# Turning v with identity products and placing half of the sums' head blocks on POOL, in a fused Mamba, cross-attention and ternary-FFN block

## The reference, cut to what matters

```python
xn   = rmsnorm(x);  proj = xn @ w_in.T                # val, gate (256 each), B, C (16 heads x 128), dt (16)
val  = silu(causal_conv4(val));  dt = softplus(dt + bias);  ld = -exp(A_log) * dt
cum  = cumsum(ld)                                     # per chunk and head
L    = exp(cum[l] - cum[m]) where l >= m, else 0
Y    = ((C @ B.T) * L) @ val_heads + D * val          # 16 heads of 16 channels
out  = (Y * silu(gate)) @ w_out.T                     # then a decayed associative memory read, residual
x    = layernorm(x + attn);  x = layernorm(x + cross_attention(x, ctx, mask))
x    = layernorm(x + bitlinear(silu(depthwise_conv3(bitlinear(x)))))
```

## Time and profile before

| | us |
|---|---|
| median of 3 runs | 879.39 (878.04 to 880.06) |
| the profiled execution, whole | 878.6 |
| its span, first to last instruction | 876.8 |
| TensorE busy in the span | 818.3 (93%) |
| VectorE, ScalarE, GpSimd busy | 723.8, 738.7, 166.3 |
| mean granted TensorE clock, share of full | 0.976 |

### The profile page before, as it was taken

One profiled execution on the slowest core, in us unless ns is written; L12 is line 12 of the kernel. 1 busy time (PEld: TensorE's weight loads), 2 busy tenths in 40 slices (PEclk: granted clock), 3 DMA queues, 4 the chain that ended last, 5 costly groups with the idle time before them and its releaser, 6 DMA issues.

```text
span 876.8 us, 19690 instructions
## 1 busy us (share of the span) xinstructions
PE 818.3 (93%) x7051; PEld 570.0 (65%) x7051; DVE 723.8 (83%) x2189; ACT 738.7 (84%) x1409; POOL 166.3 (19%) x198
## 2 busy tenths in 40 slices
PE   7789999999999999999999999999999999997784
PEld 5565766676676767676776767676767767664442
DVE  3633567989899898989898998989898998889685
ACT  3868779989898999989898989998998989694633
POOL 7101020203112030303031120303130220211110
PEclk9889999999999999999999999999999999999798
DMA  6301121203020211112020302111120302000000
GB/s 184 76 18 25 21 44 31 33 2 63 15 62 16 55 22 48 17 37 39 15 62 15 61 16 53 36 37 16 28 48 16 61 16 49 16 26 13 6 7 24
DMA packets 59261, 31.34 MB, mean 36 GB/s; under 512 B 48122, under 2 KB 50124, under 8 KB 59164
## 3 DMA queue, kind: packets, MB, share of 16 engines
q1 hardware_dynamic: 58732, 28.97, 15.1%
q10 hardware_dynamic: 432, 1.11, 0.5%
HBM read 16.68 MB, written 4.19 MB: 24 GB/s over the span
## 4 chain that ended last, share of the span: by engine, by line
PE 59%; SPq 11%; ACT 11%; DVE 9%; issue 4%; DMA 4%; POOL 0%; ACTq 0%; POOLq 0%; DVEq 0%
PE pM L2325 9%; SPq L524 9%; PE pP L2277 5%; PE pP L2278 4%; PE pP L2279 4%; DMA cum_diag<-cum 3%; PE pDec L2312 3%; PE pY L2341 3%; PE pDec L2313 2%; SPq L512 2%; PE pA L2376 2%; PE pA L2277 2%; PE pC L2408 2%; PE pD L2520 2%; PE pC L2448 2%
## 5 line engine op out<-in xcount | busy, mean ns | idle before, releaser
L2277 PE MATMUL pP<-xn_hi,G_hi 128*128 128x256 f32 x512 | 168.2, 329 | 0.3 <-DVE xn_lo L1605 0.3
L762 ACT ACTIVATE P<-pP 128x512 f32<-128x512 f32 x256 | 150.5, 598 | 17.6 <-PE pP L2279 16.1
L2278 PE MATMUL pP<-xn_lo,G_hi 128*128 128x256 f32 x512 | 144.5, 282 | 0.0
L2279 PE MATMUL pP<-xn_hi,G_lo 128*128 128x256 f32 x512 | 144.4, 282 | 0.0
L2325 PE MATMUL pM<-P,xnT 128*64 128x512 f32 x512 | 138.5, 619 | 0.5 <-DVE ML L1654 0.4
L624 POOL TENSOR_TENSOR rs_c<-ve_c,half_pow 128x4 f32<-128x4 f32 x48 | 48.7, 1014 | 436.6 <-DVE nm_c L1702 288.8
L2277 PEld LDWEIGHTS pP<-xn_hi,G_hi 128*128 128x128 f32 x512 | 97.3, 190 | 38.1 <-issue 14.5
L1654 DVE TENSOR_TENSOR ML<-pM,Lm 128x512 f32<-128x512 f32 x128 | 87.6, 684 | 32.2 <-PE pM L2325 25.4
L2278 PEld LDWEIGHTS pP<-xn_lo,G_hi 128*128 128x128 f32 x512 | 97.4, 190 | 8.4 <-issue 5.0
L771 ACT ACTIVATE Lm<-pDec 128x512 f32<-128x512 f32 x128 | 76.8, 600 | 27.6 <-PE pDec L2313 26.5
L2279 PEld LDWEIGHTS pP<-xn_hi,G_lo 128*128 128x128 f32 x512 | 97.0, 190 | 0.0
(11 more groups left out here) (242 smaller groups left out, 2009.3 us busy)
## 6 DMA issues: line engine op xcount, KB each, us to landing
v_nat<-vT SPq DMA_DIRECT2D x256, 32.0 KB, 2.1
x_in<-in_x SPq DMA_DIRECT2D x16, 256.0 KB, 4.0
x_res<-in_x SPq DMA_DIRECT2D x16, 256.0 KB, 2.7
ctxT<-in_ctx_t SPq DMA_DIRECT2D x16, 256.0 KB
cum_diag<-cum SPq DMA_DIRECT2D x256, 3.0 KB
out_x<-r SPq DMA_DIRECT2D x16, 256.0 KB, 2.1
P<-in_wc ACTq DMA_DIRECT2D x2, 512.0 KB, 7.0
P<-in_wb SPq DMA_DIRECT2D x2, 512.0 KB, 8.6
```

The costliest lines, as they stand in the source:

```text
L762: act.activation(P[:, half, 2 * pair:2 * pair + 2, 0:w], pP[k % 2][:, 0:2 * w].rearrange("p (h l) -> p h l", h=2), ACT.Copy).then_inc(p_co ...
L2277: pe.matmul(dst, w_hi, x_hi, start=True, stop=False)
L2278: pe.matmul(dst, w_hi, x_lo, start=False, stop=False)
L2279: return pe.matmul(dst, w_lo, x_hi, start=False, stop=True)
```

## The change

Three things.

First, `v_nat` and `move_v` are gone. `v_transposed(n, half)` reads `vT` itself: for each of four sequences, two channel halves jj and two positions h2 of a head in its pair, one product of 64 columns of `vT` with 64 picked columns of the identity, which turns them and picks them in one go. 16 products stand in place of 4 transposes. What waited for the transfers now waits for `vT` (PE) or for the products (ACT's `value_silu`, two groups later).

Second, the first half of `cum_diag` is written by POOL: the new `place_cum(n, 0)` makes 8 products of `cum3` with the column of `sel` that is one for the block's own heads and zero elsewhere. The second half is still moved by SP. Of SP's 32 small transfers a group 8 are left.

Third, all lists of calls are new, on every engine. In POOL's, `place_cum(g + 1, 0)` stands ahead of `stage_c_rsqrt(g - 1, 2)` and of `spread_cum(g + 1)`.

```diff
+CUM_MOVED = (1, 16 * HH)
-        v_nat = sb("v_nat", [128, GS, 2, L])
-        cum_moved = [sig(f"cum_moved{i}", 16 * HH) for i in range(2)]
+        cum_moved = [sig("cum_moved0", CUM_MOVED[0]), sig("cum_moved1", CUM_MOVED[1])]
-            def move_v(n):
-                        sp.wait_ge(vT_ready.sem, vT_ready.at(n, jj + 1))
-                        for q in range(4):
-                            for h2 in range(2):
-                                sp.dma_start(v_nat[E * hh:E * hh + E, 0:seqs_in(n), h2, :], ...)
...
             def body(g):
+                load_x(g + 1)
                 load_c(g - 1)
-                load_x(g + 1)
-                move_v(g)
-                move_cum(g, 0)
                 move_cum(g, 1)
                 store(g - 4)
...
+            def place_cum(n, half):
+                pool.wait_ge(a_read.sem, a_read.at(n, A_CT))
+                pool.wait_ge(dec_mm.sem, dec_mm.unit(FIRST_UNIT[n] + HALF * half - GS + HALF - 1))
+                mine = slice(HALF * half, HALF * half + HALF)
+                for hh in range(HH):
+                    last = pool.tensor_scalar(cum_diag[0:CUM_ROWS, mine, hh, :], cum3[:, mine, :], sel[:, hh:hh + 1],
+                                              None, ALU.mult)
+                last.then_inc(cum_moved[half].sem, 1)
...
-                act.wait_ge(v_nat_ready.sem, v_nat_ready.at(n - 2, 16 * V_MOVES))
+                act.wait_ge(a_mm.sem, a_mm.at(n - 2, A_VT + 1))
...
+            id_heads = id_f[:, :].rearrange("p (q h e) -> p h q e", q=4, h=2)
             def v_transposed(n, half):
-                pe.wait_ge(v_nat_ready.sem, v_nat_ready.at(n, 16 * V_MOVES))
+                pe.wait_ge(vT_ready.sem, vT_ready.at(n, JJ))
                 for k in range(half_seqs(n)):
                     s = HALF * half + k
-                    last = pe.transpose(bank(pA, k), flat(v_nat[:, s, :, :]), id_f[:, :])
+                    for jj in range(JJ):
+                        for h2 in range(2):
+                            last = pe.matmul(pA[64 * h2:64 * h2 + 64, 128 * k + 64 * jj:128 * k + 64 * jj + 64],
+                                             vT[n % 2][:, jj, L * s:L * s + L], id_heads[:, h2], start=True, stop=True)
```

More of the change, by code:

```diff
@@ L842, in place_cum @@
                 act.wait_ge(cum_spread.sem, cum_spread.at(n - 1, 1))
-                for moved in cum_moved:
-                    act.wait_ge(moved.sem, moved.at(n - 1, 16 * HH))
+                for moved, count in zip(cum_moved, CUM_MOVED):
+                    act.wait_ge(moved.sem, moved.at(n - 1, count))
                 act.activation(flat(cum3[:, 0:seqs_in(n), :]), pA[0:CUM_ROWS, 0:width(n) // 2].bitcast(BF16), ACT.Copy)\
@@ L2570, in fill @@
+                head_pair(0, 1, 4)
+                scores(0, 3)
+                head_pair(0, 1, 5)
+                decay(0, 4)
                 head_pair(0, 1, 6)
-                decay(0, 4)
+                project(1, A_VAL[1], 1)
                 head_pair(0, 1, 7)
-                scores(0, 3)
                 head_pair(1, 0, 0)
+                decay(0, 5)
                 head_pair(1, 0, 1)
-                project(1, A_VAL[1], 1)
-                keys(0)
-                head_values(0, 0)
@@ L2579, in fill @@
-                head_values(0, 1)
+                head_pair(1, 0, 2)
+                cum_sums(1)
+                head_pair(1, 0, 3)
+                project(1, A_GATE[0], 2)
                 head_values(0, 2)
@@ L2582, in fill @@
                 scores(0, 4)
-                cum_sums(1)
-                head_pair(1, 0, 2)
-                head_pair(1, 0, 3)
-                project(1, A_GATE[0], 2)
-                decay(0, 5)
+                project(1, A_GATE[1], 3)
                 head_pair(1, 0, 4)
-                project(1, A_GATE[1], 3)
                 head_pair(1, 0, 5)
+                scores(0, 5)
+                cum_transposed(1)
+                head_values(0, 4)
+                decay(0, 6)
                 head_pair(1, 0, 6)
-                head_values(0, 4)
@@ L2593, in fill @@
[L2593 to L2608 removed]
+                v_transposed(1, 0)
@@ L2609, in fill @@
+                scores(0, 6)
+                head_pair(1, 0, 7)
+                head_pair(1, 1, 0)
+                decay(0, 7)
+                scores(0, 7)
+                v_transposed(1, 1)
+                head_values(0, 5)
                 head_values(0, 6)
                 head_values(0, 7)
+                scores(1, 0)
+                decay(1, 0)
                 head_pair(1, 1, 1)
+                x_transposed(2)
+                context_values(0)
+                decay(1, 1)
                 scores(1, 1)
@@ L2904, in drain @@
                 ffn_up(10, 2)
+                head_pair(12, 1, 7)
                 scores(12, 3)
-                head_pair(12, 1, 7)
+                head_pair(13, 0, 0)
+                head_pair(13, 0, 1)
+                decay(12, 5)
+                ffn_up(10, 3)
+                scores(12, 4)
+                head_pair(13, 0, 2)
+                x1_transposed(11)
+                head_pair(13, 0, 3)
+                cum_sums(13)
                 head_values(12, 0)
@@ L3040, in drain @@
                 memory_read(13)
+                project(15, A_VAL[1], 1)
+                ffn_up(12, 2)
                 head_pair(14, 1, 7)
-                ffn_up(12, 2)
-                project(15, A_VAL[1], 1)
+                head_values(14, 0)
+                scores(14, 3)
                 head_pair(15, 0, 0)
-                scores(14, 3)
-                head_values(14, 0)
+                ffn_up(12, 3)
+                head_pair(15, 0, 1)
+                scores(14, 4)
                 head_values(14, 1)
```

1240 lines of the change are left out of this document (601 added, 639 removed).

## The result

| | before | after |
|---|---|---|
| median, us | 879.72 (878.04 to 880.06, 4 runs) | 908.93 (906.09 to 910.68, 4 runs) |
| ratio | | 1.0333, 95% interval 1.0302 to 1.0363 |
| the profiled execution, and its span | 878.6, 876.8 | 909.5, 907.7 |

The change makes the kernel 3.3% slower. The page's first part after, against the earlier trace rows: TensorE is busy 26 us longer (844.0 against 818.3), POOL 119 us longer.

The account below looks back on a forecast made before the run. TensorE was taken as the bound, busy 566.25 of 580 us. +16.7 (v) - 15.4 (waits) - 3.4 (fill) = -2.1 us from 878.6 gave 876.5, with the median 0.8 above: 877 us, 8 in 10 from 867 to 891.

Parts of the forecast that it names:

- It just fits, and I count no wait: First decay in the steady stretch: POOL's new path takes 13.4 us against 13.5 available, so TensorE does not wait.
- Waits for the blocks: TensorE's waits for head blocks before each group's first decay, outside the fill, go: 15.4 us gained.
- It fits too, without slack: ScalarE finishes second_apply and head pair 7's copy at 12.4 us; TensorE wants the pair at 12.5.
- POOL is late: Rival: POOL's path takes 14.5 us, 1.0 late in each of 14 groups; +14, 891 us; chance 0.22.
- v on TensorE: Turning v by TensorE products: 1.04 us a half, 1.11 us more a group; +16.7 us (+1 to +27).
- What is queued behind the blocks: POOL's square root for second_apply is ready at 10.3 us after the transposes; ScalarE loses up to 0.8 us.
- VectorE held up by POOL: Rival: qi on VectorE stalls beside POOL's blocks, 1.5 us a group, half let through; +10, 887 us; chance 0.12.
- no VectorE row grows beside POOL: Trace observation about VectorE beside POOL, with the caveat that no such qi met a long POOL product.
- The fill: Start of the kernel: first decay at 43.2 us instead of 46.66, a gain of 3.4 us; bounds nothing to 7.
- nothing, if the narrow work before it comes later: Lower bound on the fill's gain, if narrow work before it or the setup products come later.
- The order: New call lists on all engines: counted as 0, with 3 us either way.
- The sum: Whole kernel: +16.7 - 15.4 - 3.4 = -2.1 us.

Follow-up runs that it names:

- mended: Kernel after, with SyncE instead of POOL moving the first-half blocks, the weights' cast back in place, two drain stores behind the moves: 868.9 us, ratio 0.9887.
- root_sixth: weights_later with the second norm's root behind the sixth of POOL's eight blocks instead of the eighth: 891.93 us, ratio 1.0147.
- weights_later: Kernel after, with VectorE's cast of the projection weights put back behind the first head_low and split_xn: 902.53 us, ratio 1.0256.
- memsets_wait: Kernel after, with POOL's memsets of cum_diag and what follows waiting until the projection weights' cast is done: 900.68 us, ratio 1.0248.
- idle_products: mended plus 8 unread 48x256 POOL products in each of 8 steady periods, behind the third norm's root: 869.99 us, ratio 0.9891.
- place_alone: Kernel before, with only the first half of the head blocks placed by POOL instead of moved by SyncE: 979.19 us, ratio 1.1136.

## Why the prediction was wrong, step by step

**Which step failed.** The step "It just fits, and I count no wait", under "Waits for the blocks", and with it "It fits too, without slack" for `second_apply`. The rival that I called "POOL is late" is what happened in the steady stretch, and the fill went the wrong way for a reason that no case of mine had.

**v on TensorE: right.** I took 1.04 us a half; the rows give 1.03 (432.98 - 431.95). In its window the kernel before has TensorE at work for 566.25 / 12 = 47.19 us a period, mended for 578.60 / 12 = 48.22: +1.03, against +1.11 predicted.

**Waits for the blocks: wrong.** That the first decay is wanted so much later was right, as mended shows: with v's products and the new order the period is 48.3, idle time all but gone, so 1.1 us of work did stand in for 1.1 us of waiting. It was POOL that could not supply. The product was mis-sized: 0.83 us taken, 0.88 the upper estimate, 0.92 the median and 0.94 the mean measured.

```profile
L606 POOL TENSOR_SCALAR cum_diag<-cum,sel x128: 914/918/1154, 44.0 to 783.7; 48x256 bf16<-48x256 bf16 x128
```

Eight of them took 7.39 us instead of 6.6. With root and spreading POOL's path was 436.27 - 424.42 = 11.85 us against 10.9, 0.95 more than reckoned where 0.1 was to spare. It ended 436.27 - 423.75 = 12.52 us after `cum3` began, 1.2 later than the 11.30 that mended wants: close to the rival's 1.0. I had taken half of the long product's time; two sizes give the cost per element and the fixed part, (1.56 - 0.92) / 256 elements and 0.28 us fixed, and I had set the fixed part at nothing to 0.20.

**What is queued behind the blocks: wrong, and dearer.** I looked at `second_apply` and wrote that ScalarE loses up to 0.8 us. It lost 2.40 at the place shown, and 27.2 us in the twelve times between 120 and 700 us. Counted from the end of the transposes as in the prediction (422.02 in this trace), the root was ready at 11.1 instead of 10.3, and ScalarE was free for it at 8.7 instead of 9.5: the term was wrong on both sides. VectorE's figures for the root were there at 429.61, 5.9 us after `cum3` began, but the root stood behind all eight blocks and began at 431.79. root_sixth puts a number to it: with the blocks and the spreading no earlier, the root 1.85 us sooner gave 10.6 of the kernel's us. Both together, with the 2.2 us by which the first decay of all is later (44.9 against 42.7), cost the difference between weights_later and mended, 902.5 - 868.9 = 33.6 us. I priced the rival at 14, as a wait of 1.0 us at one place; it was two late results of one queue, the first of which also delays everything behind it on ScalarE. Period +2.2 us instead of +1.0.

**VectorE held up by POOL: seen, and not the loss.** Two `qi` rows a period beside the blocks took 0.70 and 0.73 us instead of 0.43, so VectorE lost 0.57 us a period there and not the 1.5 that this rival foresaw. In mended, where POOL has no blocks, a `qi` row some 10 us behind `cum3` loses 0.42 beside the spreading (the row below), and TensorE still idles for only 1.40 us of 580. So VectorE loses 0.15 us a period more than in mended, which leaves next to nothing of the 2.2 us for this rival. The Trainium skill ("SBUF — State Buffer", section "SBUF: two separate sides") has the two engines sharing a port pair under an exclusive lock with the loser blocked; the rows now agree for VectorE as the loser too. One row of before had shown it already: the cast of 1.97 us at 15.30, beside POOL's memsets, which takes 0.43 in memsets_wait. The prediction's sentence that no VectorE row grows beside POOL was wrong there. In idle_products 0.8 us of it in a period cost nothing. In the fill it cost 6 to 8 us, at a place where I did not look.

```profile
407.86 0.85 DVE L1792 TENSOR_SCALAR qi<-u 128x512 bf16<-128x512 f32 x1
```

**The fill: wrong in sign.** I reckoned from `cum3` at 33.27 and asked only what comes after it. The new lists had moved what comes before: the cast stood first on VectorE and beside POOL's memsets. Moving it gave 6.4 us, making the memsets wait 8.3. With the cast back in its place the first decay came 46.66 - 44.9 = 1.8 us sooner than before, where I had 3.4. My bound "nothing, if the narrow work before it comes later" was no bound; a fill can lose.

**The order: too little.** The lists as such gain. Of the 9.5 us by which mended's span is shorter than that of before, 4.0 are won up to the first decay and 3.0 more by that of group 3 (174.7 us before, 167.7 in mended); 1.1 are lost up to that of group 15 (755.5, 749.6), and 3.6 won from there to the end. So -5.5 came behind the first decay, where my terms (+16.7, -15.4 and 0 for the order) add up to +1.3; no run says which list made it. With SyncE in POOL's place, the cast mended and two stores moved, 877 is 8 us too high; the part of the forecast that was not about POOL was too timid.

**The sum.** -2.1 was predicted and +29 came: +33.6 for POOL's queue and +6.4 for the cast, less the 10.8 by which everything else is faster than before (879.7 - 10.8 + 33.6 + 6.4 = 908.9). The sum closes because each term is the difference of two neighbouring kernels; that it closes proves nothing more.

## What to carry to other kernels

When a slow engine takes over placing work, add up everything that stands behind it in that engine's queue until each consumer, one sum per consumer, and ask for each which neighbour queue it stalls in turn; a path that "just fits" by an estimated duration is a loss as likely as not. When lists are written anew, read the first twenty microseconds too, engine against engine: a cast moved to the front, beside memsets, cost 6 us here, and a store ahead of a transfer, in the drain, some 10. And do not throw away a slow change whole: two of its three parts were worth 1.1% once the third was undone and the cast put back.

## What the hardware showed that was not expected

- VectorE's cast of 128x512 took 0.43 us alone (memsets_wait), 2.35 when it began at 14.79 (weights_later) and 7.80 when it began at 9.30 (after) beside a row of POOL memsets. In all twelve kernels whose memsets do not wait for it, it ended at 17.0 to 17.3 us, 0.3 us behind the last memset, wherever it began: it got no turn between POOL's instructions. Not every form is held: `xn_lo`, at 14.13 in weights_later beside the same memsets, took 0.74 us as it does in after when they are over. The VectorE rows seen beside POOL's products grew by some 0.3 to 0.4 us only.
- A 48x256 product of POOL took 0.92 us, the 48x512 one 1.56: halving the elements took off 41%.
- TensorE, idle for 3.2 us in the fill until 19.2, was at 1.2 GHz from 20 to 28 us, and 3.6 us of lateness became 7.1; in place_alone a wait of 7.2 us was followed by some 5 us at half clock, and the kernel was 99.9 us slower where the waits had grown by 71.2.
